# First attention of a fused transformer kernel: queries and keys in stacked high and low parts, scores by two f32r products

## What is computed

```python
h = _L0_tok_ref(x, L0_tok_W, L0_tok_b, L0_tok_pos_embed)
h = jnp.concatenate([h, txt], axis=1)
h = h + _L0_attn_ref(_layernorm(h, axis=-1), L0_attn_Wq, L0_attn_bq, ...)
...
# _L0_attn_ref, one head of width 64, no scale:
k = jnp.einsum('bnh,oh->bno', x, Wk) + bk
v = jnp.einsum('bnh,oh->bno', x, Wv) + bv
scores = jnp.einsum('bik,bjk->bij', q, k)
attention = jax.nn.softmax(scores, axis=-1)
attended = jnp.einsum('bij,bjk->bik', attention, v)
```

## Times and profile before

| | us |
|---|---|
| median of 3 runs (5559.76, 5559.78, 5568.03) | 5559.78 |
| the profiled execution | 5535.23 |
| its span | 5533.4 |
| PE busy in the span | 4295.1 |
| DVE busy | 3325.1 |
| ACT busy | 1894.7 |
| POOL busy | 490.8 |

### The profile page before, as it was taken

The page is one execution under the profiler, slowest core; times in us unless marked ns, Lnnn a source line. Parts: engine busy times, 40 slices in busy tenths (PEclk is TensorE's granted clock), DMA queues, the critical chain, the costliest instruction groups (busy, mean ns, idle before and its releaser), DMA issues.

```text
span 5533.4 us, 72582 instructions
## 1 busy us (share of the span) xinstructions
PE 4295.1 (78%) x26536; PEld 2888.3 (52%) x26536; DVE 3325.1 (60%) x9075; ACT 1894.7 (34%) x3395; POOL 490.8 (9%) x820
## 2 busy tenths in 40 slices
PE   6886855699888855699888855699887855699987
PEld 4554634555646534555646534555646544555646
DVE  4444769555545769555545769555555769655555
ACT  2333522144332522144432522134432532234432
POOL 0110000011100000021100000021100000021100
PEclk9898865699988975699988975689998985699988
DMA  2000000000000000000000000000000000000000
GB/s 81 3 3 16 1 16 1 1 1 1 1 1 4 1 16 1 1 1 1 1 1 4 1 16 1 1 1 1 1 1 4 1 1 1 1 1 1 1 1 4
DMA packets 28333, 26.68 MB, mean 5 GB/s; under 512 B 10550, under 2 KB 26934, under 8 KB 27450
## 3 DMA queue, kind: packets, MB, share of 16 engines
q1 hardware_dynamic: 27962, 21.98, 1.4%
HBM read 20.40 MB, written 1.57 MB: 4 GB/s over the span
## 4 chain that ended last, share of the span: by engine, by line
PE 52%; DVE 30%; POOL 4%; issue 2%; ACT 2%; DVEq 1%; SPq 0%; POOLq 0%; ACTq 0%
PE ps L594 11%; PE ps L630 7%; DVE qup L779 4%; PE ps L657 4%; PE ps L1624 3%; PE ps L1608 3%; DVE x L777 3%; DVE x L781 3%; DVE ctxt L822 3%; DVE ctxt L818 3%; POOL st L395 2%; PE ps L935 2%; PE ps L597 2%; DVE row_max L1067 2%; PE ps L964 2%
## 5 line engine op out<-in xcount | busy, mean ns | idle before, releaser
L630 PE MATMUL ps<-cst,big 128*128 128x128 f32 x4608 | 659.5, 294 | 308.9 <-ACT big L733 251.7
L630 PEld LDWEIGHTS ps<-cst,big 128*128 128x128 f32 x4608 | 567.0, 152 | 366.2 <-ACT big L733 255.7
L713 ACT COPY big<-ps 128x512 f32<-128x512 f32 x816 | 478.5, 586 | 742.4 <-PE ps L630 739.6
L737 ACT ACTIVATE big<-ps,negmax 128x1024 f32<-128x1024 f32 (+1 forms) x672 | 600.1, 899 | 265.7 <-DVE negmax L852 265.7
L852 DVE TENSOR_REDUCE negmax<-ps 128x1 f32<-128x1536 f32 x336 | 590.4, 1758 | 64.6 <-PE ps L601 44.8
L410 PE MATMUL ps<-cst 128*128 128x512 f32 x608 | 334.2, 710 | 127.9 <-DVEq L187 58.2
L594 PE MATMUL ps<-kup,qup 128*128 128x512 f32 (+3 forms) x768 | 355.2, 559 | 41.9 <-POOLq L187 41.1
L395 POOL TENSOR_TENSOR st<-st,cst 128x6 f32<-128x6 f32 x104 | 156.9, 1508 | 2579.5 <-DVE st L383 2575.4
L423 ACT COPY xt<-ps 64x512 f32<-64x512 f32 x144 | 78.4, 580 | 808.6 <-PE ps L415 808.5
L601 PE MATMUL ps<-qlo 128*128 128x512 f32 x576 | 337.9, 725 | 7.5 <-DVEq L187 7.5
L657 PE MATMUL ps<-big,v 128*32 128x128 f32 (+1 forms) x8064 | 321.9, 277 | 8.1 <-DVE ctxt L1091 6.0
(11 more groups left out here) (318 smaller groups left out, 7201.9 us busy)
## 6 DMA issues: line engine op xcount, KB each, us to landing
rw<-in_w_route SPq DMA_DIRECT2D x128, 64.5 KB, 1.9
cst<-in_consts SPq DMA_DIRECT2D x1, 2671.0 KB, 14.9
cst<-in_consts SPq DMA_DIRECT2D x1, 2670.5 KB, 8.9
big<-in_consts SPq DMA_DIRECT2D x1, 1872.5 KB, 22.1
out_dram<-res SPq DMA_DIRECT2D x4, 384.0 KB, 2.8
experts_in<-in_consts SPq DMA_DIRECT2D x1, 1360.0 KB, 17.6
qup<-in_patches SPq DMA_DIRECT2D x4, 260.0 KB
klo<-in_pe_low SPq DMA_DIRECT2D x2, 384.0 KB, 23.6
```

What stands on the lines that cost most here:

```text
L630: ins = nc.tensor.transpose(turned_bank(kind, u, g)[:, i * P:(i + 1) * P], prob[:, slot_of(kind, u), (4 * g + i) * P:(4 * g + i + 1) * P], ...
L713: copy(pt[:, slot_of(kind, u), g, 0:n], turned_bank(kind, u, g)[:, 0:n]).then_inc(*ph.mark(copier(kind, g)))
L737: nc.scalar.activation(prob[:, slot_of(kind, u), cols], src[:, cols], ACT.Exp, bias=bias, accum_out=part_sum[:, u, k:k + 1]).then_inc(*ph. ...
```

## The change

Queries and keys are written as a high part, which is the value rounded to f32r, and a low part, the difference between the value and its high part. `q_stack[:, 0]` holds the high part of the queries in partitions 0 to 63 and the low part in 64 to 127. `k_stack[:, 0]` holds the high part of the keys twice, once in each half, and `k_stack[:, 1]` the low part twice. The score of a bank is then the sum of two f32r products over 128 partitions, with `k_stack[:, 0]` and with `k_stack[:, 1]`.

To have each projection twice, DVE lays the query and key weights down twice side by side in `twice` (part of `big`) at the start of embed, so that each projection product has 128 output rows. Queries and keys alternate, one block of 512 tokens after the other. ACT writes the high parts of all six blocks, DVE the low parts. The clearing of the upper half of `qlo` by POOL is left out of embed. All other passes stay.

```diff
+        twice = big[:, 0:2 * P].rearrange("p (w r d) -> p w r d", w=2, r=2)
...
-        def qkv_pe(ph, pe, wq, wk, wv):
+        def qkv_blocks():
+
+            return [(w, j) for j in range(NB) for w in range(2)]
+
+        def qkv_pe(ph, pe):
             keep_clock(1, 9)
             pe.wait_ge(*ph.after("normed", 1))
             transpose_pe(ph, x, [0, 1, 2])
-            for j in range(NB):
+            pe.wait_ge(*ph.after("weights_spread", 2))
+            for i, (w, j) in enumerate(qkv_blocks()):
                 pe.wait_ge(*ph.after("xt_copied", j + 1))
-                nc.tensor.matmul(ps[0:D, 3 + j, :], W(wq), xt[:, 512 * j:512 * (j + 1)], start=True, stop=True)\
-                    .then_inc(*ph.mark("q_psum"))
-            for j in range(NB):
-                nc.tensor.matmul(ps[0:D, (6 + j) % 8, :], W(wk), xt[:, 512 * j:512 * (j + 1)], start=True, stop=True)\
-                    .then_inc(*ph.mark("k_psum"))
-            rows_pe(ph, W(wv), xt, [1, 2], "v_psum")
+                nc.tensor.matmul(ps[:, (3 + i) % 8, :], twice[:, w, :, :].rearrange("p r d -> p (r d)"), xt[:, 512 * j:512 * (j + 1)], start=True, stop=True)\
+                    .then_inc(*ph.mark("stack_psum"))
+            rows_pe(ph, W("v0"), xt, [1, 2], "v_psum")
 
         def qkv_act(ph, act):
             transpose_act(ph, act, xt, [0, 1, 2])
-            for j in range(NB):
-                act.wait_ge(*ph.after("k_psum", j + 1))
-                nc.scalar.copy(kt[0:D, 512 * j:512 * (j + 1)], ps[0:D, (6 + j) % 8, :])
-
-        def qkv_vec(ph, dve, scale):
-            for j in range(NB):
-                dve.wait_ge(*ph.after("q_psum", j + 1))
-                nc.vector.tensor_scalar(qt[0:D, 512 * j:512 * (j + 1)], ps[0:D, 3 + j, :], scale, None, ALU.mult)
+            for i, (w, j) in enumerate(qkv_blocks()):
+                act.wait_ge(*ph.after("stack_psum", i + 1))
+                nc.scalar.activation((q_stack, k_stack)[w][:, 0, 512 * j:512 * (j + 1)].bitcast(F32R), ps[:, (3 + i) % 8, :],
+                                     ACT.Identity).then_inc(*ph.mark("high_ready"))
+
+        def qkv_vec(ph, dve):
+            for i, (w, j) in enumerate(qkv_blocks()):
+                cols = slice(512 * j, 512 * (j + 1))
+                dve.wait_ge(*ph.after("high_ready", i + 1))
+                if w == 0:
+                    ins = nc.vector.scalar_tensor_tensor(q_stack[D:P, 0, cols].bitcast(F32R), ps[D:P, (3 + i) % 8, :], 1.0,
+                                                         q_stack[D:P, 0, cols], ALU.mult, ALU.subtract)
+                else:
+                    ins = nc.vector.scalar_tensor_tensor(k_stack[:, 1, cols].bitcast(F32R), ps[:, (3 + i) % 8, :], 1.0,
+                                                         k_stack[:, 0, cols], ALU.mult, ALU.subtract)
+                ins.then_inc(*ph.mark("low_ready"))
...
+                elif kind == "attn0":
+                    for part in range(2):
+                        ins = nc.tensor.matmul(bank, q_stack[:, 0, qs].bitcast(F32R), k_stack[:, part, lo * P:hi * P].bitcast(F32R),
+                                               start=(part == 0), stop=(part == 1))
...
-                clear_upper(ph, pool)
...
+                for w, name in enumerate(("q0", "k0")):
+                    nc.vector.tensor_copy(twice[:, w, :, :], W(name).unsqueeze(1).to_broadcast([P, 2, D]))\
+                        .then_inc(*ph.mark("weights_spread"))
                 dve.wait_ge(patches_in, 32 * (b + 1))
                 nc.vector.tensor_copy(h[:, TP:T, :], txt_in)
```

More of the change, by code:

```diff
@@ L51 @@
 SIGNALS = {
-    "embed": {"pool_step": 1, "rstd_ready": 2, "xt_copied": 3, "emb_psum": 1, "xt_psum": 3, "q_psum": 3, "k_psum": 3,
+    "embed": {"weights_spread": 2, "rstd_ready": 2, "xt_copied": 3, "emb_psum": 1, "xt_psum": 3, "stack_psum": 6, "high_ready": 6, "low_ready": 6,
         "v_psum": 2, "vec_step": 13, "var_ready": 2, "normed": 1},
@@ L1394, in _ @@
                 ins.then_inc(*ph.mark("emb_psum"))
-                qkv_pe(ph, pe, "q0", "k0", "v0")
+                qkv_pe(ph, pe)
                 ph.leave(pe)
@@ L1676, in _ @@
                 ready_vec(ph, dve)
-                qkv_vec(ph, dve, 1.0)
+                qkv_vec(ph, dve)
                 ph.leave(dve)
```

## The result

| | before | changed | ratio, 95% interval |
|---|---|---|---|
| first comparison, median us (4 and 4 runs) | 5559.77 | 5504.75 | 0.9898 (0.987 to 0.9927) |
| second comparison, median us (13 runs of before, 3 of e2 below) | 5552.15 | 5498.41 | 0.9900 (0.9877 to 0.9922) |
| profiled execution: span, us | 5533.4 | 5487.2 | |
| first loop in that execution, us | 498.08 | 446.27 | |

The changed kernel is faster by 1.0%: 55.0 us in the medians of the first comparison, 53.7 in the second, and 50 in the mean of the first loops, where the whole change lies. A median of 5506 was forecast. The first loop's end is read at the first instruction of route0 on the vector engine, the reduction into `r0s`.

What follows compares the result with a forecast made beforehand. The tensor engine was taken to bound attn0; steady units 46.1 plus head 8.1 minus weight copies 0.35 gave 53.9 us less, from the median 5559.78 to a predicted 5506 us, range 5484 to 5524.

Steps and rivals of the forecast that it cites:

- What bounds attn0: Steady attn0: tensor engine busy all 43.00 of 43 us at granted clock 1.00, so it is the bound.
- The price of an f32r record: attn0 scores: 0.214 us per f32r record inside a run, against 0.43 for f32; unit falls from 5.77 to 4.49 us.
- the lower end I had given with 0.236: attn0 units: at 0.236 us per f32r record, at least 1.15 us saved per unit, over 36 units.
- the premise of 0.214: attn0 scores: an f32r record needs half the passes of an f32 record, so 0.214 us instead of 0.43.
- The steady units and the head: attn0: units 1 to 9 save 46.1 us over four rows; the start of each row saves 8.1 us over four.
- the mechanism named, the scalar engine's chain: attn0 head: unit 1's exponential follows the scalar engine's copies, moving up only 1.28 us; unit 1's transposes start 2.0 us sooner.
- Slack of the other engines: attn0: other engines can keep 3.41 us per unit; the closest race, a vector engine copy, holds by 0.7 us.
- Preparation, memset, weight copies: embed: projections and memset removal worth nothing; two added weight copies cost about 0.35 us in all, bound 0 to 0.6.
- The clock: attn0 head: about 2 us of tensor engine idle time before unit 0 is on the safe side; nothing booked.
- the rival: attn0 head: clock falls after 2 us idle, costing 2.6 to 4 us a row, total 5516 to 5522; chance 0.08.
- The fall in the steady part: Steady attn0: clock falls if transposes do not count as activity; total about 5587 at half the units; chance 0.04.
- The sum: Whole kernel: 46.1 + 8.1 - 0.35 = 53.9 us less than before.

Runs made afterwards that it cites:

- e2: Changed kernel run again without an edit, profiled and timed: median 5498.41 us over 3 fast runs, first loop 446.68 us.
- e4: Changed kernel with one f32r product per score bank, low part of the keys left out (3 records per unit): attn0 unit 3.89 us.
- e5: Changed kernel with three f32r products per score bank, low part of the keys added twice (9 records per unit): attn0 unit 5.29 us.
- e8: Changed kernel with two extra unused copies of 0.68 us ahead of each real copy of turned group 1 in attn0: unit 5.06 us.
- e7: Changed kernel with one extra unused copy ahead of each real copy of turned group 1 in attn0: unit 4.59 us, first loop 448.53 us.
- e3: Changed kernel's stacks, but each score bank formed by one f32 product without the keys' low part: ratio to before 0.9996, unit 5.77 us.
- e6: Kernel before with the memset of the query and key buffer's upper half moved ahead of the first loop: ratio to before 1.0009.
- e1: Kernel before run again without an edit and profiled: span 5548.7 us, first loop 494.81 us.

## Why the prediction was right, point by point

**What bounds attn0.** Right. The tensor engine is busy throughout at 1.00 before and after, and e4 shows that it still binds at 3.89.

**The price of an f32r record.** This term was mis-sized: 0.214 taken, 0.233 measured by the line of e4, the changed kernel and e5. The unit came to 4.59, not 4.49, and saves 1.18, not 1.28. Over the 36 steady units that is 42.5 us rather than 46.1, close to the lower end I had given with 0.236. That an f32r record is half of an f32 record, the premise of 0.214, is shown by no run; of the two values at hand the wrong one was taken into the sum.

**The steady units and the head.** The first profile's scores of a row begin at 74.85, and its last addition of attn0 is followed by mean0's first reduction at 135.21: 60.36 us, where before it was 147.10 - 74.32 = 72.78. That is 12.4 us in the first row, 49.7 for four such rows, and the unit starts of the other three rows lie equally far apart; forecast were 46.1 + 8.1 = 54.2. Unit 1 came 1.89 us sooner (2.0 forecast) by the mechanism named, the scalar engine's chain; the step to unit 2 saved 1.1.

**Slack of the other engines.** Right: 0.7 us computed, 0.7 to 0.8 by e8, and e7's copy fitted in.

**Preparation, memset, weight copies.** Right within what can be measured, and in the first row two copies of 0.36 us together where 0.35 was booked. The ratios of e3 and e6 bound it to some 0.2% (10 us), their first loops (497.79 and 497.50 against 498.08 and 494.81) more closely. That the copy into h is covered was read from one embed at the lower clock level; at the upper one, in one embed of e1, the memset cost some 0.4 us.

**The clock.** Half wrong. The step that failed is the one that called 2 us of idle time safe, on the ground of one gap of 2.28 us with a fast follower. The runs show no such line: the clock fell in none of 24 heads at 0.65 and 1.19 us, in 3 of 20 at 1.85 and in 3 of 4 at 2.54. The price is small (1.1 us in the head of e2's first row, so less than 1 us per launch in the mean), and the rival, with 2.6 to 4 us in every row, had it too dear and too frequent. The fall in the steady part did not come: the clock of the stretch is 1.00, with transposes in 1.47 of every 4.59 us.

**The sum.** Forecast 53.9 us less. The first loops give 51.8 in the two first profiles and 50.0 over the four, the medians 55.0 and 53.7. The forecast median 5506 against 5504.75 is partly luck: the terms were some 4 us too large, and the medians move by more than that from one comparison to the next (before: 5559.77 and 5552.15; changed: 5504.75 and 5498.41).

## What to carry to other kernels

When a stage is bound by one engine, its period can be predicted by subtracting records from the unit (here to 2%), but the price of a record should come from records of the same type and shape in the same trace, behind the first of a run, not from halving another type's. Before subtracting two spans, compare a part of the program that the change can't touch; here that part moved by more than a third of the gain between executions. A step that is covered by more than its length can be left alone. The cover can be computed from one timeline (0.7 us computed, 0.7 to 0.8 measured), as long as the clock is the same; where it differs between executions, as in embed, the cover moves with it.

## What the runs showed of the hardware

- An f32r record of 512 columns costs 0.233 us at the upper clock level, where an f32 record costs 0.428; the first record of a run costs 0.1 us more in either type.
- A break in a run of score records, by the join, costs about 0.045 us, with f32r and with f32 alike.
- After idle times of 1.85 us the transposes were slowed by a fallen clock in 3 of 20 heads, after 2.54 us in 3 of 4; with two filling products in none of 4.
- A copy of 128x256 in f32 on the vector engine took 2.52 us beside a GpSimd memset of 2.65 us, and 0.29 us with the memset out of the loop (e6).
- The passes that no edit touches took from 5035.3 to 5071.5 us in the profiles, a spread of 36 us over the whole study, with mean granted clocks of the whole span between 0.827 and 0.835. That the clock makes part of such differences is shown only in the first loop (mean0 and embed above). Whether it accounts for this spread stays open.
